# A two-pass adjacency kernel: h of a strip in one piece, and half of the next but one strip's sums ahead of it

## What is computed

```python
# layer 0
e = concat(par * (diag * x_users @ W_u) + x_users, par * (diag * x_items @ W_i) + x_items)
h = adj @ (adj.T @ e)
x = layernorm(x + layernorm(h) * gamma + beta + x)
# layer 1
deg = adj.sum(axis=0) + 1
z = rsqrt(deg) * (x @ W)
o = relu(rsqrt(deg) * (adj.T @ z + z) + b)
x = layernorm(x + o)
```

## Time and profile before

| what | value |
|---|---|
| median of 3 runs | 608.97 us |
| profiled execution, its own time | 609.2 us |
| its span, first to last instruction | 607.4 us |
| mean granted clock of TensorE | 0.995 |
| TensorE matmul busy | 578.3 us, 4648 instructions |
| VectorE busy | 346.3 us |
| ScalarE busy | 178.5 us |
| POOL busy | 115.2 us |
| DMA, mean over the span | 337 GB/s |

### The profile page before, as it was taken

One profiled execution on the slowest core, in us unless ns is written; L12 is line 12 of the kernel. 1 busy time (PEld: TensorE's weight loads), 2 busy tenths in 40 slices (PEclk: granted clock), 3 DMA queues, 4 the chain that ended last, 5 costly groups with the idle time before them and its releaser, 6 DMA issues.

```text
span 607.4 us, 10911 instructions
## 1 busy us (share of the span) xinstructions
PE 578.3 (95%) x4648; PEld 219.9 (36%) x4648; DVE 346.3 (57%) x464; ACT 178.5 (29%) x432; POOL 115.2 (19%) x166
## 2 busy tenths in 40 slices
PE   9979999999999999999999999999999999877794
PEld 6423333333333333333333334544433334222232
DVE  3996676878868676986766694555520004400026
ACT  2035080633618062351807148334000001000001
POOL 3007052250706132050504114101000000000000
PEclk9989999999999999999999999999999999999998
DMA  9999796969788795978889597799999999999992
GB/s 312 386 377 363 249 350 223 389 221 354 269 307 319 260 386 190 384 270 307 287 287 387 187 391 271 293 399 378 422 421 422 421 419 422 420 420 423 412 387 101
DMA packets 77401, 204.82 MB, mean 337 GB/s; under 512 B 4126, under 2 KB 6686, under 8 KB 68136
## 3 DMA queue, kind: packets, MB, share of 16 engines
q1 hardware_dynamic: 76288, 203.27, 88.6%
q10 hardware_dynamic: 1064, 0.84, 0.4%
HBM read 202.79 MB, written 1.31 MB: 336 GB/s over the span
## 4 chain that ended last, share of the span: by engine, by line
PE 79%; DMA 14%; SPq 3%; DVE 2%; ACT 1%; issue 0%; DVEq 0%
PE psum L876 32%; PE psum L969 24%; PE psum L1056 14%; DMA turned<-in_adj_dram 7%; PE psum L977 5%; DMA slot<-in_adj_dram 4%; SPq L308 3%; DMA last_slot<-in_adj_dram 3%; PE psum L1076 1%; PE psum L931 1%; PE psum L1034 1%; PE psum L943 1%; SPq L312 0%; DVE slot L699 0%; DVE C L751 0%
## 5 line engine op out<-in xcount | busy, mean ns | idle before, releaser
L693 DVE STREAM_TRANSPOSE slot<-slot 128x2048 f32<-128x2048 f32 x80 | 178.1, 2281 | 68.4 <-PE psum L876 68.4
L876 PE MATMUL psum<-slot,E 128*64 128x512 f32 x800 | 180.0, 597 | 1.2 <-DMA slot<-in_adj_dram 0.7
L969 PE MATMUL psum<-slot,T 32*64 32x512 f32 x2560 | 144.1, 596 | 3.3 <-DVE T L674 3.3
L1056 PE MATMUL psum<-slot,E 128*64 128x512 f32 x480 | 106.2, 594 | 11.2 <-DMA slot<-in_adj_dram 11.0
L876 PEld LDWEIGHTS psum<-slot,E 128*64 128x64 f32 x800 | 54.4, 137 | 113.0 <-issue 108.8
L422 POOL COPY turned<-last_slot 32x1024 f32<-32x1024 f32 x80 | 84.1, 1052 | 38.9 <-issue 31.2
L969 PEld LDWEIGHTS psum<-slot,T 32*64 32x64 f32 x2560 | 55.9, 133 | 89.5 <-issue 82.1
L483 ACT ACTIVATE turned<-last_slot 32x1024 f32<-32x1024 f32 x80 | 84.3, 1054 | 5.3 <-DVE last_slot L693 3.6
L817 DVE TENSOR_TENSOR T<-psum,dinv 128x256 f32<-128x256 f32 x10 | 4.2, 424 | 134.5 <-PE psum L1076 134.0
L1056 PEld LDWEIGHTS psum<-slot,E 128*64 128x64 f32 x480 | 35.2, 137 | 79.1 <-issue 78.9
L475 ACT ACTIVATE T<-turn 32x186 f32<-32x186 f32 (+4 forms) x200 | 53.5, 309 | 21.2 <-DVE turn L668 19.0
(11 more groups left out here) (112 smaller groups left out, 273.1 us busy)
## 6 DMA issues: line engine op xcount, KB each, us to landing
slot<-in_adj_dram SPq DMA_DIRECT2D x152, 1024.0 KB, 14.2
last_slot<-in_adj_dram SPq DMA_DIRECT2D x30, 1024.0 KB, 7.8
turned<-in_adj_dram SPq DMA_DIRECT2D x9, 1024.0 KB, 16.1
X<-in_x_dram SPq DMA_DIRECT2D x5, 256.0 KB, 4.4
turned<-in_adj_dram SPq DMA_DIRECT2D x2, 512.0 KB, 12.1
out_dram<-T ACTq DMA_DIRECT2D x6, 128.0 KB, 7.0
out_dram<-T SPq DMA_DIRECT2D x4, 128.0 KB, 2.6
beta_b<-in_L_gnn_ln_beta_dram SPq DMA_DIRECT2D x1, 32.0 KB, 11.6
```

What stands on the lines that cost most here:

```text
L693: v.transpose(parts, parts).then_inc(chunk_cut, 1)
L876: return mm(acc[half[b % 2], :], E[:, b, :], view[:, b % CB, :], start=(b < 2), stop=(b >= NB - 2))
L969: last = mm(acc[half[h], a, :], T[step % 2][rows_a, jb, d, :], slot[step % 2][rows_a, h:NF:2, :, cols], start=step == 0 and jb == 0 and d ...
L1056: last = mm(bank[ACC[RES + n // NB * WIDE + s]][half[b % 2], :], E[:, b, :], wide[i % PLACES][:, s * JW:(s + 1) * JW], start=(b < 2), stop ...
```

## The change

t of a strip is no longer cut in two around h. In a step, h of all four jb runs in one piece. After it, t of the next strip is finished, and then, for steps 0 to 7, the first five chunks of t of the strip after that are summed in a second PSUM bank (`t_acc` is bank 5 or bank 6 by the step's parity). `AHEAD[s]` is how many chunks of the strip of step s + 1 are summed before h of step s: 1 for strip 1 (ahead of the first h), 5 for the strips of steps 2 to 9, none behind. VectorE cuts these chunks after chunks 8 and 9 of the strip before. The copies into T are regrouped: the four own copies (d = 0) of each engine come first, h of jb 0 starts when these are done, and the others are waited for ahead of its d = 1. The small matmul for `mirrored` comes behind h of step 0, and its copy on VectorE (`copy_mirrored`) behind the cut of the one chunk ahead. Everything after step 9 is as it was.

```diff
-COPIES = [(a, f, d, n) for f in range(2) for a in range(4) for d, n in ((0, 4 - a), (4 - a, a)) if n]
-DVE_COPIES, ACT_COPIES = COPIES[0:8], COPIES[8:14]
+OWN_COPIES = [[(a, f, 0, 4 - a) for a in range(4)] for f in range(2)]
+OTHER_COPIES = [(a, f, 4 - a, a) for f in range(2) for a in range(1, 4)]
+COPIES = OWN_COPIES[0] + OWN_COPIES[1] + OTHER_COPIES
+DVE_COPIES, ACT_COPIES = OWN_COPIES[0] + OTHER_COPIES[0:4], OWN_COPIES[1] + OTHER_COPIES[4:6]
+OWN = 4
+ACT_ALL = len(ACT_COPIES) + len(COPIES)
...
+AHEAD = [1] + [NQ // 2] * (NJ - 2) + [0]
...
-        t_acc = bank[5]
+        t_acc = [bank[5], bank[6]]
...
             for step in range(NJ):
-                for q in range(NG - 2 if step == 0 else 0, NF):
+                for q in range(NG - 2 if step == 0 else AHEAD[step - 1], NF):
                     cut_chunk(step * NQ + q)
                 turn_t(step, 0)
                 spread_t(step)
...
                 if step == 0:
                     mirror_norm()
+                for q in range(AHEAD[step]):
+                    cut_chunk((step + 1) * NQ + q)
+                if step == 0:
+                    copy_mirrored()
...
             def h_group(step, jb):
 
                 for d in range(4):
+                    if jb == 0 and d == 1:
+                        pe.wait_ge(spread_dve, (step + 1) * len(DVE_COPIES))
+                        pe.wait_ge(spread_act, step * ACT_ALL + len(ACT_COPIES))
                     for a in range(4):
...
-                acts = len(ACT_COPIES) + len(COPIES)
-                pe.wait_ge(spread_dve, (step + 1) * len(DVE_COPIES))
-                pe.wait_ge(spread_act, step * acts + len(ACT_COPIES))
+                pe.wait_ge(spread_dve, step * len(DVE_COPIES) + OWN)
+                pe.wait_ge(spread_act, step * ACT_ALL + OWN)
...
                 h_group(step, 1)
-                if step == 0:
-                    pe.wait_ge(gamma_ready, 1)
-                    mm(mirrored, WM[:, 1, :], centre[:, :], start=True, stop=True).then_inc(norm_mirrored, 1)
-                if not final:
-                    pe.wait_ge(t_summed, 2 * (step + 1))
-                    t_pairs(step + 1, 0, HS // 2)
-                pe.wait_ge(spread_act, (step + 1) * acts)
+                pe.wait_ge(spread_act, (step + 1) * ACT_ALL)
                 h_group(step, 2)
                 h_group(step, 3).then_inc(slots_used if not final else h_done, 1)
                 if final:
                     return
-                t_pairs(step + 1, HS // 2, HS)
+                if step == 0:
+                    pe.wait_ge(gamma_ready, 1)
+                    mm(mirrored, WM[:, 1, :], centre[:, :], start=True, stop=True).then_inc(norm_mirrored, 1)
+                t_pairs(step + 1, 2 * AHEAD[step], HS)
+                if AHEAD[step + 1]:
+                    pe.wait_ge(t_summed, 2 * (step + 1))
+                    t_pairs(step + 2, 0, 2 * AHEAD[step + 1])
                 pe.wait_ge(moved_act, (step + 1) * len(ACT_MOVES))
                 pe.wait_ge(moved_pool, (step + 1) * len(POOL_MOVES))
...
+            t_pairs(1, 0, 2 * AHEAD[0])
             for step in range(NJ):
                 h_step(step)
```

More of the change, by code:

```diff
@@ L464, in copy_t @@
                     act.wait_ge(spread_dve, step * len(DVE_COPIES))
-                    act.wait_ge(spread_act, step * (len(ACT_COPIES) + len(COPIES)))
+                    act.wait_ge(spread_act, step * ACT_ALL)
                 for i in range(2):
                     cols = slice(i * HW, (i + 1) * HW)
-                    nc.scalar.activation(t_sum[:, cols], t_acc[half[1], cols], ACT.Copy).then_inc(t_half_copied, 1)
+                    nc.scalar.activation(t_sum[:, cols], t_acc[step % 2][half[1], cols], ACT.Copy).then_inc(t_half_copied, 1)
             def spread_T(step):
@@ L665, in turn_t @@
                 dve.wait_ge(t_half_copied, 2 * step + i + 1)
-                v.tensor_tensor(cols, t_acc[half[0], i * HW:(i + 1) * HW], cols, ALU.add).then_inc(t_summed, 1)
+                v.tensor_tensor(cols, t_acc[step % 2][half[0], i * HW:(i + 1) * HW], cols, ALU.add).then_inc(t_summed, 1)
                 dve.wait_ge(t_summed, 2 * step + i + 1)
@@ L680, in mirror_norm, with copy_mirrored @@
                 v.tensor_scalar(centre[:, :], centre[:, :], gamma_col[:, 0:1], None, ALU.mult).then_inc(gamma_ready, 1)
+            def copy_mirrored():
                 dve.wait_ge(norm_mirrored, 1)
@@ L883, in first_sums @@
                 for b in range(q * CB, (q + 1) * CB):
-                    last = sweep(t_acc, chunk(0, q), b)
+                    last = sweep(t_acc[0], chunk(0, q), b)
                 last.then_inc(chunk_summed if q < NQ - 1 else t_done, 1)
@@ L954, in t_pairs @@
                     for b in (2 * p, 2 * p + 1):
-                        last = sweep(t_acc, chunk(step, q), b)
+                        last = sweep(t_acc[step % 2], chunk(step, q), b)
                     if p == HS - 1:
```

## The result

The changed kernel takes 626.74 us in the median of four runs (624.97 to 627.65) against 609.51 for the kernel before on the same chip: a ratio of 1.0278, with a 95% interval from 1.0254 to 1.0302. It is slower by 17.2 us. The forecast was 617.9 with a range to 625.5, so the direction was right and the size too small by about nine microseconds. The profiled execution took 627.65 us, with a span of 625.9.

A forecast was written before the change was run, and what follows sets the result against it. TensorE was taken as the bound, busy 578.3 of 607.4 us. 607.4 - 3.2 - 3.6 + 15.7 = 616.3 span; 1.8 around it and 0.2 off give 617.9 us, range 608.5 to 625.5.

The forecast's parts named there:

- Joints: Strip steps 0 to 8: each loses one h piece and one t piece on TensorE, together -3.2 us.
- The start: Before the first h: a strip 1 chunk fills TensorE's gap, h starts earlier and the slow clock is avoided, -3.6 us.
- Costed at nothing: Strip steps: t_summed wait, T of the next strip, VectorE's cuts, SyncE's order, mirrored wait and matmul were taken to cost 0.
- Rival 4: Strip steps: copies of T or cuts late on VectorE, 14 us, with loads half as late: 624 us; chance 0.03.
- Rival 1: Slot loads run at 422 GB/s and are in time, so the kernel gets faster: 602.4 us; chance 0.10.
- rival 2: Only the undisturbed lateness of slot loads counts, 0.9 to 1.3 us in seven steps: 608.7 to 611.5 us; chance 0.16.
- Rival 3: TensorE's clock falls at every stall in seven steps, adding 12 us: 630 us; chance 0.05.
- The late load: Chunks further on wait for slot loads: 2.2 us a step in steps 1 to 7, 0.3 in step 0, +15.7 us.
- second cost: Two last_slot loads queued ahead of the slot burst make its fifth load land 0.5 us later a step.
- The burst's own share: Fifth slot load, a step: 0.9 us late even undisturbed, plus 0.7 for unevenness between bursts.
- the 9.1 us case: Slow last_slot loads land 9.1 us after issue instead of 7.5, making the fifth slot load up to 1.6 us later.

The follow-up runs named there:

- the pair with three chunks: Changed kernel with three chunks further on instead of five, with and without the one chunk ahead of the first h: 603.53 us with it, 606.90 us without.
- the kernel with less to load: Changed kernel, but from step 2 on the slot loads of chunks 0 to 4 bring only two of four rows a partition: 603.73 us, ratio 0.9907.
- k3_again: Changed kernel with three chunks further on instead of five, measured a second time: 603.53 us, ratio 0.9891 to the kernel before.
- k3: Changed kernel with three chunks further on instead of five, first measurement: 603.66 us, ratio 0.9914 to the kernel before.

## Why the prediction was right or wrong

**Joints, -3.2.** Right: 0.33 us a step by the pieces, 3.0 in nine steps, and 13.92 for h in one piece.

**The start, -3.6.** Right in size where it can be seen alone (3.4 us by the pair with three chunks), wrong for the shown execution of the changed kernel: there the load landed at 40.2 instead of 38.8, the gap was 2.62 us instead of 1.2, and the clock fell although I had given it back. With the same order of loads it lands at 38.8 to 40.6 in thirteen profiles, so I had taken the earliest. The clock is a matter of the single execution: it fell at the first h in two of the ten profiles with the chunk ahead, and in three of the four without it, so the chunk does seem to help, though not each time.

**Costed at nothing.** Right: the kernel with less to load has every other part of the change and its steps are as long as the pieces. Rival 4 (copies and cuts late) is out. It appears only with no chunk further on. Rival 1 (loads in time at 422 GB/s) and rival 2 (0.9 to 1.3 us) are out by the measured stall of 3.1. Rival 3 (the clock falls at every stall) did not come: the granted clock is 1.00 over all seven stalled steps.

**The late load, +15.7.** The mechanism was right: the waits of L889 for loads of slot, their return in each of the steps 1 to 7, the issue of last_slot 9.25 us after the start of h in the mean (forecast 9.3), and the burst 4.6 behind it in the step shown (forecast 4.7). Step 0, for which I had added 0.3, shows no wait.

Only the size was off, and the term that failed is the "second cost" that "comes from the queue": put at 0.5 us a step and measured at 1.4. The burst's own share, 0.9 + 0.7 = 1.6 in the prediction, measured 1.7. I had taken the second last_slot load at its shortest time to landing, 7.5 us, and set the 9.1 us case aside as "up to 1.6 more". By the profile of the changed kernel it was issued when I said, but took 8.6 us in the mean of the seven steps (7.6 to 10.1), and landed 17.3 to 20.1 us after the start of h, 18.5 in the mean, instead of 17.45. The fifth load of slot follows it by 13.5 to 14.8 us, 13.9 in the mean; I had 13.4 and 0.7 for unevenness, which was enough. Together that is a fifth landing 32.4 us after the start of h and a want at 29.4: 3.0 late, where I had 2.1. The mean over steps 1 to 8 of the kernel before is 8.0 and not 7.5, so half of the error could have been read there; the other half could not.

The account of the miss: the span was forecast at 616.3 and measured at 625.9, 9.6 more. The stall (3.11 instead of 2.2, seven times) is 6.4 of it and the start 3.3; the joints (0.2 less than forecast) and step 0 (0.3 the other way) nearly cancel.

Why single loads come 1 to 2 us late was not tried. The traces show a coincidence and no more. The page counts transfers of another queue among those of this core:

```profile
q8 instruction: 37, 0.61, 0.4%
```

In three of the seven steps the second last_slot load lands 3.8 to 4.1 us behind the first instead of 2.7, and one of these 37 transfers starts within 1.2 us of the first one's landing (at 174.9, 214.3 and 327.1). In a fourth step the first last_slot load itself takes 8.1 us instead of 5.5 to 6.2, with such a transfer at 283.5, while it is under way. But others lie beside loads that were on time (at 94.8, for one).

The range failed for the same reason: its upper end was built from a stall of 3.2 us together with the full gains of the start.

## What to carry to other kernels

When work is pulled ahead, ask for every buffer when it is released and when its refill is first wanted: here h in one piece released the slots at one moment, and the fifth load was wanted 9 chunks of work later however the chunks were divided, so the number of loads needed by then decides and not the depth of prefetch. Cost a load by what is queued ahead of it, with mean and not shortest times to landing, for each link of the queue; here both terms that missed, the second last_slot load and the first load of strip 1, had been read from one early landing. And try the small depth first: two chunks cover what VectorE needs, five cost 3.9% more than two (ratios to the kernel before 1.0278 and 0.9892).

## What the runs showed of the hardware that was not expected

The length of TensorE's gap before the first h did not decide by itself whether the clock fell. In one profile with three chunks (k3_again) a gap of 1.96 us was followed by a granted clock of 0.50, and in the profile with only the regrouped copies a gap of 3.09 us was followed by h at full speed, 7.13 us for two blocks. The timeline and one window of the first:

```profile
39.94 3.56 PE L889 MATMUL psum<-slot,E 128*64 128x512 f32 x8 [1.96 <-DMA slot<-in_adj_dram]
```
```profile
41.00:42.00 1.00, 1.00 (x4) 0.30 (x2) 0.90 (x4) 0.50 (x2) 0.00 (x0) 0.50 1.07 391
```

And of the second:

```profile
40.80 7.13 PE L976 MATMUL psum<-slot,T 32*64 32x512 f32 x128 [3.09 <-DVE T L678]
```
```profile
42.00:43.00 1.00, 1.00 (x25) 0.45 (x17) 1.00 (x2) 0.85 (x3) 0.57 (x4) 1.00 1.06 391
```

In the first, two gaps of 0.24 and 0.81 us came shortly before; in the second one of 0.81. What decides was not found. It does differ between executions of one kernel: k3 is the same program as k3_again, and in its profile the clock stayed at 1.00, the chunk took 1.94 us instead of 3.56, and the first h started at 41.16 instead of 43.43 (0.65 us of this because the load landed sooner). So executions of one kernel differ by some 1.7 us for the clock alone, and a single profile is a weak judge of the start.
